# A fused attention and expert kernel: row maxima over two banks, value products in twos, normalising on GpSimd

## The reference, cut to what matters

```python
# x: (8, 56, 128) tokens; ctx: (8, 1500, 128) context; 16 heads of 8 dims
x = x + mha(ln(x), ln(x))                 # self attention, 56 keys
x = x + mha(ln(x), ln(ctx))               # pass 0: cross attention, 1500 keys, ctx normalised
x = x + moe(ln(x))                        # 8 experts, top 2, 128 -> 512 -> 128, gelu
x = x + mha2(ln(x), ctx)                  # pass 1: cross attention, 1500 keys, ctx as it is,
                                          #         weights quantised to three values
# each mha: softmax(q k^T / sqrt(8)) v per head, then the output projection
```

## Time and profile before

| | us |
|---|---|
| median of 3 runs | 704.53 (701.89 to 708.60) |
| the profiled execution's span | 702.3 |
| PE busy | 575.3 |
| DVE busy | 419.9 |
| ACT busy | 330.4 |
| POOL busy | 151.9 |

### The profile page before, as it was taken

How to read it: one execution, slowest core, us unless ns; L and a number is a source line. 1 busy time by engine, 2 the same in 40 slices (tenths; PEclk the granted TensorE clock), 3 DMA queues, 4 the chain that set the end, 5 groups by cost and what they waited for, 6 DMA issues and landing times.

```text
span 702.3 us, 17085 instructions
## 1 busy us (share of the span) xinstructions
PE 575.3 (82%) x6582; PEld 390.0 (56%) x6582; DVE 419.9 (60%) x1090; ACT 330.4 (47%) x495; POOL 151.9 (22%) x128
## 2 busy tenths in 40 slices
PE   1798645499979797999969859366989999999996
PEld 0677333266656565676736637233646657557674
DVE  5657567389868686867234201565746676766730
ACT  0264214156747373765733213213546666666572
POOL 1563112114131323210015000121121312302000
PEclk9899659599989898999988979766979999999997
DMA  4010947555939393854200841129757696695500
GB/s 151 19 45 17 126 90 91 85 89 91 134 58 128 61 121 61 101 76 60 90 1 30 133 89 60 25 58 127 116 69 127 84 146 101 92 149 77 68 2 14
DMA packets 25197, 57.24 MB, mean 82 GB/s; under 512 B 4532, under 2 KB 8748, under 8 KB 25140
## 3 DMA queue, kind: packets, MB, share of 16 engines
q1 hardware_dynamic: 25140, 56.45, 51.6%
HBM read 17.81 MB, written 0.23 MB: 26 GB/s over the span
## 4 chain that ended last, share of the span: by engine, by line
PE 34%; DMA 24%; issue 21%; DVE 9%; SPq 7%; POOL 2%; ACT 1%; DVEq 0%; ACTq 0%; POOLq 0%
DMA cx<-in_ctx 14%; DMA xT<-in_ctxT 7%; PE SM L1168 6%; PE PO L1183 5%; SPq L377 5%; PE ST L1147 5%; DVE mxp L790 4%; PE MI L1099 4%; PE MI L1089 3%; PE MI L1123 2%; DMA qall<-qsplit 2%; PE SM L1255 1%; DMA kst<-ksplit 1%; SPq L384 1%; PE SM L1123 1%
## 5 line engine op out<-in xcount | busy, mean ns | idle before, releaser
L790 DVE TENSOR_REDUCE mxp<-SM 112x1 f32<-112x500 f32 x364 | 238.1, 673 | 85.1 <-PE SM L1168 84.2
L592 ACT ACTIVATE PT<-ST 128x896 f32<-128x896 f32 x192 | 174.9, 912 | 71.5 <-PE ST L1147 70.7
L1168 PE MATMUL SM<-kst,qst 96*112 96x500 bf16 x364 | 150.4, 418 | 39.2 <-DVE mxp L790 27.4
L1183 PE MATMUL PO<-PT,vaug 125*32 125x112 f32 x3072 | 116.5, 270 | 1.7 <-ACT PT L592 1.5
L1147 PEld LDWEIGHTS ST<-qst,kst 98*128 98x128 bf16 x1536 | 96.2, 102 | 38.3 <-issue 19.4
L1147 PE MATMUL ST<-qst,kst 98*128 98x112 bf16 x1536 | 111.5, 217 | 1.3 <-DMA qst<-mrow 1.1
L470 POOL TENSOR_TENSOR kr<-kf,ksplit 128x500 f32<-128x500 f32 x48 | 55.5, 1159 | 211.4 <-ACT ksplit L564 211.3
L1183 PEld LDWEIGHTS PO<-PT,vaug 125*32 125x32 f32 x3072 | 69.0, 111 | 43.7 <-issue 38.7
L1168 PEld LDWEIGHTS SM<-kst,qst 96*112 96x112 bf16 x364 | 48.7, 134 | 79.3 <-DVE mxp L790 43.6
L475 POOL TENSOR_TENSOR ksplit<-kr,ksplit 128x500 bf16<-128x500 f32 x48 | 54.4, 1135 | 79.0 <-DVE ksplit L785 79.0
L576 ACT ACTIVATE vaug<-MI 125x512 f32<-125x512 f32 x48 | 28.7, 598 | 80.8 <-PE MI L1099 80.8
(11 more groups left out here) (129 smaller groups left out, 565.6 us busy)
## 6 DMA issues: line engine op xcount, KB each, us to landing
kst<-ksplit SPq DMA_DIRECT2D x192, 187.5 KB, 7.3
cx<-in_ctx SPq DMA_DIRECT2D x8, 750.0 KB
xT<-in_ctxT SPq DMA_DIRECT2D x8, 750.0 KB, 9.2
moe<-in_w1T SPq DMA_DIRECT2D x8, 256.0 KB, 6.3
moe<-in_w2T SPq DMA_DIRECT2D x8, 256.0 KB, 7.0
qall<-qsplit SPq DMA_DIRECT2D x12, 112.0 KB, 5.4
watt<-in_watt SPq DMA_DIRECT2D x1, 768.0 KB, 6.2
qst<-mrow SPq DMA_DIRECT2D x32, 1.8 KB
```

The source lines that it names most:

```text
L592: nc.scalar.activation(PT[:, k % 2], ST[:, k % 2, :, 0:4 * PC], ACT.Exp, scale=SCALE).then_inc(exp_done, 1)
L790: nc.vector.tensor_reduce(mxp[:, j // 3, j % 3:j % 3 + 1], tile_bank(j, banks), AX.X, ALU.max).then_inc(sm_red, 1)
L1168: mm(tile_bank(j, banks), qst[n.par][0:SROWS, j // 3], kst[n.par][0:SROWS, j // 3, at:at + THIRD], start=True, stop=True).then_inc(sm_full, 1)
L1183: last = mm(PO[32 * p:32 * p + 32, PC * half:PC * (half + 1)], vaug[n.par][:, c, at:at + 32], PT[0:KC, k % 2, cc, PC * p:PC * (p + 1)], st ...
```

## The change: what it does

- The 24 max tiles of a unit become 12 pairs (`MAXES`). A pair's two tiles go to the two banks of `SM` (in `start_pass` also to two banks of `ST`), and one `tensor_reduce` reads both banks and writes two columns of `mxp`. In a window a pair waits for the reduce of the pair before it. Each step has one pair; the first window of a pass has 15 in all.
- `values` of steps k-2 and k-1 are issued together at even k; `PT` has four buffers instead of two.
- The transposes of the next unit's maximum move from step 6 to 8, and from 8 to 10 in a pass's first window.
- `ctx_normalise` of units 3 to 7 moves to POOL, behind `k_parts`; DVE waits for the previous unit's before it writes the statistics anew.
- The loops over windows are written out.

```diff
@@ constants @@
+PTB = 4
-START_TILES = 18
-STEP_TILES = spread_tiles(0, (3, 3, 3, 2, 2, 2, 2, 2, 1, 1, 2, 1))
-OWN_MX_STEP, NEXT_MX_STEP = 1, 6
-FIRST_TILES = spread_tiles(TILES - START_TILES, (3, 3, 3, 3, 2, 2, 3, 3, 2, 2, 2, 2))
-FIRST_OWN_MX_STEP, FIRST_NEXT_MX_STEP = 3, 8
+MAXES = TILES // 2
+START_MAXES = 9
+STEP_MAXES = spread_maxes(0, (1,) * STEPS)
+OWN_MX_STEP, NEXT_MX_STEP = 1, 8
+FIRST_MAXES = spread_maxes(MAXES - START_MAXES, (2, 2, 1, 1, 1, 1, 1, 1, 1, 1, 2, 1))
+FIRST_OWN_MX_STEP, FIRST_NEXT_MX_STEP = 3, 10
-def run_windows(eng, s, window):
-
-    window(Unit(s, None, 0))
-    with eng.Fori(0, 2) as it:
-        window(Unit(s, it, 1))
-        window(Unit(s, it, 2))
-    for u in range(5, B):
+def run_windows(s, window):
+
+    for u in range(B):
         window(Unit(s, None, u))
-        PT = sb("PT", [128, 2, 2, 4 * PC])
+        PT = sb("PT", [128, PTB, 2, 4 * PC])
+        def max_banks(j, pairs):
+
+            if j % pairs < pairs - 1:
+                return ST[0:PC, 1, :, 0:THIRD]
+            return SM[0:PC, :, 0:THIRD]
@@ gpsimd @@
+            def ctx_normalise(n):
+
+                pool.wait_ge(crstd_ready, n.count(1, 1))
+                for i in range(3):
+                    for c in range(CPT * i, CPT * (i + 1)):
+                        last = nc.gpsimd.tensor_scalar(cx[n.par][:, c], cx[n.par][:, c], cmv[:, c, 0:1],
+                                                       crstd[:, c:c + 1], ALU.subtract, ALU.mult)
+                    last.then_inc(cn_ready, 1)
+
             def window(n):
                 ln_unit = n + 3 if n.s == 0 and (n + 3).exists() else None
                 if (n + 2).exists():
                     k_parts(n + 2, ln_unit)
+                if ln_unit is not None:
+                    ctx_normalise(ln_unit)
@@ scalar @@
-                wait(act, pv_done, n.count(STEPS, k - 1))
-                nc.scalar.activation(PT[:, k % 2], ST[:, k % 2, :, 0:4 * PC], ACT.Exp, scale=SCALE
+                wait(act, pv_done, n.count(STEPS, k + 1 - PTB))
+                nc.scalar.activation(PT[:, k % PTB], ST[:, k % 2, :, 0:4 * PC], ACT.Exp, scale=SCALE
@@ vector @@
+            def reduce_maxes(n, j, pairs=1):
+
+                dve.wait_ge(sm_full, n.count(MAXES, j + 1))
+                nc.vector.tensor_reduce(mxp[:].rearrange("q p i -> q (p i)")[:, 2 * j:2 * j + 2],
+                                        max_banks(j, pairs), AX.X, ALU.max).then_inc(sm_red, 1)
@@ vector, window @@
-                    tiles = n.tiles(k)
-                    if tiles:
+                    maxes = n.maxes(k)
+                    if maxes:
...
-                        reduce_tile(n + tiles[0][0], tiles[0][1])
+                        reduce_maxes(n + maxes[0][0], maxes[0][1])
                         if k == 0 and not n.first():
                             max_parts(n, 1)
+                        if maxes[0] == (0, MAXES - 1):
+                            max_parts(n, 1)
+                        if maxes[0] == (1, MAXES // 2 - 1):
+                            max_parts(nxt, 0)
...
                         if k == 5:
+                            if ln_unit.it is not None or ln_unit.c > 3:
+                                dve.wait_ge(cn_ready, (ln_unit + -1).count(3, 3))
                             ctx_aggregate(ln_unit)
-                        if k in (7, 8, 9):
-                            ctx_normalise(ln_unit, (k - 7,))
@@ tensor @@
-            def max_tile(n, j, banks=2):
+            def max_tiles(n, j, pairs=1):
...
-                wait(pe, sm_red, n.count(TILES, j + 1 - banks))
-                at = THIRD * (j % 3)
-                mm(tile_bank(j, banks), qst[n.par][0:SROWS, j // 3], kst[n.par][0:SROWS, j // 3, at:at + THIRD],
-                   start=True, stop=True).then_inc(sm_full, 1)
+                wait(pe, sm_red, n.count(MAXES, j + 1 - pairs))
+                for i in range(2):
+                    p, at = (2 * j + i) // 3, THIRD * ((2 * j + i) % 3)
+                    last = mm(max_banks(j, pairs)[:, i], qst[n.par][0:SROWS, p], kst[n.par][0:SROWS, p, at:at + THIRD],
+                              start=True, stop=True)
+                last.then_inc(sm_full, 1)
@@ tensor, window @@
                     scores(n, k)
-                    tiles = [(n + ahead, j) for ahead, j in n.tiles(k)]
-                    if tiles:
-                        max_tile(*tiles[0])
-                    if k:
-                        values(n, k - 1)
-                    elif prv.exists():
-                        values(prv, STEPS - 1)
-                    for tile in tiles[1:-1]:
-                        max_tile(*tile)
+                    maxes = [(n + ahead, j) for ahead, j in n.maxes(k)]
+                    if maxes:
+                        max_tiles(*maxes[0])
+                    if k % 2 == 0 and (k or prv.exists()):
+                        of = n if k else prv
+                        values(of, (k - 2) % STEPS)
+                        values(of, (k - 1) % STEPS)
...
-                    if len(tiles) > 1:
-                        max_tile(*tiles[-1])
+                    if len(maxes) > 1:
+                        max_tiles(*maxes[1])
```

More of the change, by code:

```diff
@@ L110, in first, with maxes @@
         return self.it is None and self.c == 0
-    def tiles(self, k):
+    def maxes(self, k):
         if not (self + 1).exists():
             return []
-        return FIRST_TILES[k] if self.first() else STEP_TILES[k]
+        return FIRST_MAXES[k] if self.first() else STEP_MAXES[k]
     def mx_steps(self):
@@ L682, in _ @@
             start_pass(0)
-            run_windows(act, 0, window)
+            run_windows(0, window)
             finish_pass(0)
@@ L705, in _ @@
             start_pass(1)
-            run_windows(act, 1, window)
+            run_windows(1, window)
             finish_pass(1)
@@ L855, in window @@
                             place_q(k_unit, 0)
-                        for ahead, j in tiles[1:]:
-                            reduce_tile(n + ahead, j)
-                            if not ahead and j == TILES - 1:
-                                max_parts(n, 1)
-                        if (1, TILES // 2 - 1) in tiles:
-                            max_parts(nxt, 0)
+                        for ahead, j in maxes[1:]:
+                            reduce_maxes(n + ahead, j)
                     if 0 <= k - K_STEP - 1 < 3 and k_unit.exists():
@@ L953, in start_pass @@
                 place_q(first, 0)
-                for j in range(START_TILES):
-                    reduce_tile(first, j, banks=4)
-                    if j == 3:
+                for j in range(START_MAXES):
+                    reduce_maxes(first, j, pairs=2)
+                    if j == 1:
                         place_q(first, 1)
-                    if j == START_TILES - 2:
+                    if j == START_MAXES - 1:
                         place_q(first + 1, 0)
-                    if j in (1, 4, 7):
-                        k_second_part(first + 1, j // 3)
-                    if j == TILES // 2 - 1:
+                    if j in (0, 2, 3):
+                        k_second_part(first + 1, (0, 2, 3).index(j))
+                    if j == MAXES // 2 - 1:
                         max_parts(first, 0)
@@ L1311, in start_pass @@
                 first = Unit(s, None, 0)
-                for j in range(START_TILES):
-                    max_tile(first, j, banks=4)
-                    if j in (1, 4, 7):
-                        prev = project_v(first, j // 3, prev)
-                    if s == 0 and j in (10, 13, 16):
-                        prev = transpose_ctx(first + 2, (10, 13, 16).index(j), prev)
-                    if j == TILES // 2 + 3:
+                for j in range(START_MAXES):
+                    max_tiles(first, j, pairs=2)
+                    if j in (0, 2, 3):
+                        prev = project_v(first, (0, 2, 3).index(j), prev)
+                    if s == 0 and j in (5, 6, 8):
+                        prev = transpose_ctx(first + 2, (5, 6, 8).index(j), prev)
+                    if j == MAXES // 2 + 1:
                         transpose_max(first, 0)
@@ L1325, in finish_pass @@
                 k_unit = Unit(1, None, 0) if s == 0 else None
+                values(last, STEPS - 2)
                 values(last, STEPS - 1)
```

38 lines of the change are left out of this document (15 added, 23 removed).

## The result

| | before | after |
|---|---|---|
| median (lowest to highest), us | 704.0 (701.9 to 708.6) | 716.9 (716.4 to 718.6) |
| profiled span | 702.3 | 716.8 |
| TensorE, VectorE, GpSimd busy | 575.3, 419.9, 151.9 | 567.2, 395.9, 199.6 |
| granted clock, mean | 0.891 | 0.889 |

The change makes the kernel slower: ratio 1.020, 95% interval 1.016 to 1.024, on four runs each. The prediction was 720 us, in a range of 704 to 731.

What follows compares the result with a forecast made beforehand. Most windows were taken to run at TensorE's issue order, lengthened by waits. Pass 0 +8.1, pass 1 +7.6 and loops -0.3 gave +15.4 on the 702.3 us span, 717.7; with the median's 2.2 offset 720 us, range 704 to 731.

Steps and rivals of the forecast that it cites:

- The stall of the pairs: In steps 7, 9 and 11 TensorE waits 0.8 to 1.0 us for the pair's reduce; second halves gain 2.9 us.
- Windows 0 and 1 of pass 1: The later transposes in the pass's first window make xT late: +3 us, between 2 and 4.7.
- The start passes: Nine pairs over four banks with VectorE the limit: -0.5 us in each pass.
- Window 1 of pass 0: Later transposes in the first window delay cx, VectorE waits in step 1: +3.1 us, between 1 and 4.
- The three cx windows: Steady first-pass windows waiting for cx: +0.2 us each from its later issue, +0.6 in all.
- From landing to step 5 I keep the 9.5 us of before: In cx windows, the time from cx landing to step 5 was taken as unchanged at 9.5 us.
- rival (a): Faster: pairs save hand-overs and stalls vanish if the reduce lies beside other TensorE work; 693 us, chance 8%.
- GpSimd: Context normalising at 0.5 us an instruction on GpSimd; up to 0.75 costs nothing, upper end 1.16 with +5 us.
- Values in pairs: In each pass's last window, without max tiles, paired values free TensorE's order: -1 us a pass, between 0 and -2.
- Loops: Writing out two loops of two trips saves waits at back edges: -0.3 us in all, between 0 and -1.
- The shift in steady windows: Transposing at step 8 delays the next load, but little comes of it: cx at 23.3 us, inside 24.5.
- (c): Stalls of 1 us pull TensorE's clock to 0.90, ten windows gain 2.8 us each: 748 us, chance 5%.

Runs made afterwards that it cites:

- experiment 4: The changed kernel with the maxima of a pass's first window transposed at step 8 again instead of 10: 712.4 us, ratio 1.017 to the kernel before.
- Experiment 13: The changed kernel with pairs kept in place, but each tile reduced and its bank handed over by itself: 711.4 us, ratio 1.013 to the kernel before.
- 11: The changed kernel with maxima transposed as early as before (steps 6 and 8), pairs kept: 712.4 us, ratio 1.015 to the kernel before.
- 12: The changed kernel with single, evenly spread max tiles and maxima transposed as early as before: 700.3 us, ratio 0.996 to the kernel before.
- Experiment 3: The changed kernel with context normalising back on VectorE, all else kept: 712.3 us, ratio 1.018 to the kernel before.
- experiment 1: The changed kernel with single max tiles spread two a step instead of pairs, late transposes kept: 714.8 us, ratio 1.022 to the kernel before.
- 14: The kernel before with even single tiles, values in pairs and loops written out, normalising on VectorE: 690.4 us, ratio 0.982 to the kernel before.
- Experiment 5: The kernel before with its single max tiles spread evenly, two a step, maxima still transposed at step 6: 694.9 us, ratio 0.983.
- 6: The kernel before with loops written out and context normalising on GpSimd: 694.3 us, ratio 0.982.
- experiment 7: The kernel before with values of two steps issued together and four PT buffers, nothing else: 702.7 us, ratio 0.997.
- experiment 8: The kernel before with its loops written out, nothing else: 702.4 us, ratio 0.995.
- 2: The kernel before with single max tiles spread evenly and the next unit's maximum transposed at step 8 instead of 6: 699.2 us, ratio 0.995.

## Why the prediction was right, and where it was not

- **The total: near by luck.** One term was 12.1 us too high, the others together 11.3 too low, as the points below tell.
- **The stall of the pairs: right, in mechanism and size.** Reduce 1.20 us: 1.197. Pair to pair 1.93: 1.92. Waits of 0.83, 0.97 and 0.97 behind steps 7, 9 and 11: 0.75, 0.90 and 0.99. The sum went from pair to pair and gave the second half 15.1 us; cut at the exps it is 13.7, and the first half is 14.5 for 12.6. About 1 us of both is the stall behind step 11, which falls into the next window's first half. Whole windows: window 6 of pass 1 +2.1 for +2.1, windows 2 to 5 of pass 1 +4.3 for +4.0. Window 6 of pass 0 took +3.7, 1.6 more than I gave it; its stretch at half clock is nearly all of that, as the same window takes 26.1 us in experiment 4, where there is none. Experiment 13 shows the cause, and 11 against 12 the price of the pairs, 12 us.
- **Windows 0 and 1 of pass 1: the number near, the mechanism absent.** I took +3 for a late xT. The changed kernel doesn't wait for xT in that pass. Window 0 grew by 3.8 us (34.8 to 38.6), and takes 35.4 in experiment 13: so 3.2 of it is the pairs' joint hand-over again, which the sum left out there. Window 1 fell by 1.5, as the kernel before waits 2.97 us for xT in it and runs at half clock behind that.
- **The start passes: -0.5 each isn't there.** From the last window of pass 0 to the first of pass 1, the kernels with joint pairs (the change, 3, 4, 11) take 136.8 to 137.8 us, those with single tiles (before, 1, 12, 14) 134.9 to 135.6. The pairs cost 1 to 3 us in this piece; where in it wasn't followed up.
- **Window 1 of pass 0: right in cause, too small.** I took +3.1 for the late cx; up to step 5 of that window it was +6.2, against +2.6. The step that failed is the last: "the window is late by that". Behind this longer wait the clock was granted 0.54, which the sum left out though it had "at half clock" for the work ahead of it. Experiment 4 takes 6.2 us back. Experiment 3 takes 4.0 back there with GpSimd's part alone undone, so the late shift may not be the only cause.
- **The three cx windows: wrong.** "From landing to step 5 I keep the 9.5 us of before" is the step that failed. It was 7.4 (263.10 to 270.5), and cx landed 22.6 us after kst's issue, not the 24.5 that I kept, though my own working gave 23.3. I treated the old 34 us cycle as load time plus fixed work; part of that work was slow because of the wait itself (0.52 of the clock behind it in the kernel before, 1.00 in the changed one). With the tiles spread evenly the wait all but goes (0.27 to 1.45 us for 3.9 to 4.0), and the cycle is 30. -11.5 us where I had +0.6, and I had given rival (a) 2 us for this. Experiment 5 shows that the spread alone is enough for it, 3 that GpSimd isn't needed; 6 shows that GpSimd's normalising alone is enough as well. Why the load itself takes less is open.
- **GpSimd: in the bounds, above the value taken.** 797 ns an instruction for 0.5; my own limit of what is free was 0.75. It costs 1.1 us in each such second half (experiment 3), visible in the ledger as +2.2 for +1.1. The Trainium skill ("GPSIMD Engine Reference", 3.1 Elementwise) led to an estimated 0.19 us beside dispatch for 128 elements; the whole instruction takes 797 ns in the trace, so most of it is something that this estimate leaves out. Its advice to leave elementwise work to VectorE holds in this kernel's even versions (14 against 12), not in the kernel before (6).
- **Values in pairs: -1 us in a last window isn't there** (experiment 7: 13.5 for 13.4). The step that failed is "pairing frees TensorE's order there": in the kernel before TensorE is busy 13.1 of that window's 13.5 us and waits 0.24 us for exp, so there was nothing to free.
- **Loops: small, and not settled.** I had 0 to 1 us; experiment 8 gives 0.1 to 0.9%, which is 0.7 to 6 us. No stall at a back edge is seen to go; the sooner load in its profile is of the size by which that execution lies under its kernel's median.
- **The shift in steady windows: right, for a reason that I named only in part.** With pairs no cost of it shows (11 against 4). With quick windows it costs 1.2% (5 against 2). So the slack that I found for it isn't there once the windows are quick.
- **Rivals.** (a) fails as said: in odd steps only 0.40 us of other work lies between pairs. The rule of the Trainium skill ("VectorE: DVE Perf Modes", Rules for kernel authors) to save operations, not semaphores, which it gives for chained VectorE operations, would have it faster; here 192 fewer reduces and half the semaphores made it slower, 1.7% between experiments 11 and 12. (c) needed stalls of 1 us to pull the clock: windows 2 to 6 of pass 1 ran at 1.00 with such stalls, but three half windows did not, and were 1.4 to 2.8 us longer. So (c) was wrong for its 28 us, and right for a small part of the loss.

## What to carry to other kernels

Before two small operations are merged into one, count the buffers: where both buffers of a double buffer go into the one operation, the double buffer is gone, and the engines take turns. It costs the operation's length plus two hand-overs, less whatever other work lies between, step by step; two half-size operations on the same buffers left waits of only 0.16 to 0.25 us here (experiment 13). One tile at each end of a step did better still than two in a row (22.4 us a window for 23.7). And a wait for a load on the path is no fixed part of a cycle: it hides other delays and makes new ones, so that a cut elsewhere may give nothing (experiment 1) and a mere reordering may take the whole wait away (experiment 5).

## What the runs showed of the hardware

- A wait of 3 to 5 us for a load was followed in these traces by a stretch near the 1.2 GHz level (granted 0.50, 0.52 and 0.54 in the three stretches shown; 0.75 to 0.83 over the half window); waits of 1 us, several in a window, left it at 1.00 in windows 2 to 6 of the changed kernel's pass 1, and were followed by 0.50 for 3.4 to 6.8 us in three other half windows of it. So 2 us of a load's landing decided over 5.7 us of a half window.
- GpSimd's tensor_scalar with two per-partition operands on 125x128 f32 takes 797 ns, VectorE's 361.
- VectorE's row maximum of 1000 columns over two banks takes 1197 ns, of 500 columns 673: 1.05 ns a column and about 0.15 us fixed.
- VectorE's 48 casts of ksplit take 666 ns on average in the changed kernel for 406 before, 637 in experiment 13 with its short reduces, and 406 to 438 with single tiles. The trace shows what they meet. Casts that no work of GpSimd overlaps take 0.39 to 0.41 us in both kernels. From window 2 of pass 0 on, those of the changed kernel that begin 0.07 to 0.95 us behind the start of GpSimd's last step on the keys (L470) all end 0.27 to 0.28 us after it, and so take 0.68 to 1.34 us. One cast of either kind in window 4 of pass 1, and the GpSimd instruction:

```profile
612.58 0.41 DVE L791 CAST ksplit<-kr 128x500 bf16<-128x500 f32 x1
614.79 1.14 POOL L470 TENSOR_TENSOR ksplit<-kr,ksplit 128x500 bf16<-128x500 f32 x1
614.87 1.34 DVE L791 CAST ksplit<-kr 128x500 bf16<-128x500 f32 x1 [0.53 <-POOL kr L465]
```

So the new order moved the casts onto GpSimd's instructions. The long reduce isn't needed for it, as experiment 13 has the slow casts too.
